# VectorE takes up four kinds of work one step later in the attention stage with heads of width 64

## The chip, the cores and the metric

The kernel runs on one core of one Trainium2 chip. The metric is the device time of the launch in microseconds; the number given for a kernel is the median of its runs.

## The reference, cut to what matters

The program computes two decoder layers on `x`, four sequences (batches) of 512 tokens of width 256. Each layer is an attention, a cross attention and a mixture of experts, each added to its input and normalised. The change lies in the fifth of these six stages, the second layer's cross attention over `ctx_1024`, with 16 heads of width 64:

```
q = (x @ Wq).reshape(b, n, 16, 64)
k = (context @ Wk * 64 ** -0.5).reshape(b, m, 16, 64)
v = (context @ Wv).reshape(b, m, 16, 64)
attn = softmax(einsum('bihd,bjhd->bhij', q, k))
out = einsum('bhij,bjhd->bihd', attn, v).reshape(b, n, 1024) @ Wo + bo
x = layernorm(x + out)
```

Four batches and 512 queries, 512 keys each.

## The kernel before, in words

The stage is the function `cross_heads`. It goes through 4 batches x 16 heads x 4 tiles of 128 rows, so 256 *steps* `s`, 64 to a batch (`STEPS`). Each engine has its own instruction list, written by its own loop `for s in range(FIRST, LAST)`, and works it off in order. Engines meet only at semaphores. Within a step the order of an engine's work is the order of the blocks in its loop.

A product in float32 quality is made of three passes over operands that are split in two: `hi` is the value rounded by ScalarE as it copies it, `lo` is what VectorE finds by subtracting `hi` from the value. The pairs are `srcp` (the batch's x, turned), `ctxp` (the context), `V_hi`/`V_lo`, and for each head `qs`, `q2`, `ks`, `k2`.

What TensorE (PE) does in step s, in this order (lines 1940 to 2006): the 128x512 tile of scores whose row maxima are wanted (L1955, "max(s)", into two banks in turn); the transposed scores of step s - 7 (L1965, L1966); the weighted sum of step s - 10, three matmuls (L1979 to L1981); every fourth step a transpose of four columns of maxima (L1990); and then work that comes at few steps of a batch only:

- turning x, two chunks, at steps 56 and 57 of the batch before (L1910, "turn(0)" and "turn(1)"), bank SPARE
- the products for V, `VALUES` (L1904): two at step 0 and two at step 2 (one in SPARE, one in ROW_BANK), then one each at steps 9, 10, 16, 17 in SPARE
- the products for q (steps 3, 11, ..., 59, bank SPARE) and for k (steps 5, 13, ..., 61, bank ROW_BANK) of the next two heads (L1904)
- the output product with Wo, `OUTS` (L1937), in SPARE, half of the heads and half of the rows at a time: at steps 58, 65, 88 and 89 counted from the batch's start, so at steps 58 of the batch and 1, 24 and 25 of the next

SPARE and ROW_BANK are one PSUM bank each, so the next product in a bank waits for VectorE to have taken the one before: `PE.wait_ge(SPARE.free, SPARE.use(...))`. The transpose L1990 goes to ROW_BANK too.

ScalarE (ACT) makes in a step the two exponentials of step s - 7 (L2043, L2047), then every fourth step the copies `raw` (L2055) and `rowbuf` (L2062), then the `hi` parts: context (L2068, at step 54), x (L2073), V (L2080), q and k (L2090, L2092).

GpSimd (POOL) subtracts `hi` from the exponentials (L2198, one in every step), copies q (L2204), and at steps 46 to 49 adds the bias (L2210).

VectorE (DVE) has in step s, in this order (lines 2104 to 2184): the row maxima of max(s) (L2111), which wait for PE's matmul; `V_lo` (L2123); `ctxp` low (L2127); `srcp` low (L2132); the low parts of q and k (L2141, L2144); the reciprocal (L2151, steps 1, 5, 9, ...); the scaling of the attention by it, `attT` (L2159, steps 0, 4, 8, ...); the addition of an output product to `summed` (L2169); the statistics and the normalisation of the layer.

Before the change, VectorE takes up V_lo, ctxp low, srcp low and the addition L2169 in the same step in which PE and ACT produce what they read. VectorE's list then waits there, ahead of max(s + 1). The step is chosen by one number, `of_batch(s, r)`, which gives the batch for which s is step r.

PE starts a head's first max matmul (L1955, j == 0) once half of its q and k low parts (`SPARE.free_at`, `ROW_BANK.free_at`), POOL's copy of q and a DMA of ks (L2243, issued by SP) are done.

Of the kernel before, what the change touches and what calls it, by code (L numbers as in the profile page):

```python
# [121 lines left out]
def plain(ap):  # L122
    return ap.bitcast(f32)
# [1686 lines left out]
def cross_heads(kit):  # L1810
# [11 lines left out]
    STEPS = H1 * TB  # L1822
# [4 lines left out]
    with ExitStack() as ph:  # L1827
# [51 lines left out]
        def place(u):  # L1879
            return u // STEPS, u // TB % H1, u % TB  # L1880

        def of_batch(s, r):
            b, x = divmod(s - r, STEPS)
            return b if x == 0 and 0 <= b < B else None
# [214 lines left out]
        def dve():  # L2099
# [4 lines left out]
            for s in range(FIRST, LAST):  # L2104
                if 0 <= s < END:
                    b, h, j = place(s)
# [10 lines left out]
                        V.wait_ge(weighed.sem, weighed[u - NHI])  # L2117
                    V.tensor_tensor(STp[u % NHI][1], ST[u % NFULL], plain(STp[u % NHI][0]), ALU.subtract).then_inc(low["dve"].sem, low["dve"].inc(u))
                for r, t, n, bk in VALUES:
                    b = of_batch(s, r)  # L2120
                    if b is not None:
                        V.wait_ge(v_high.sem, v_high[b, t, n])
                        V.tensor_tensor(V_lo[:, t, n * N:(n + 1) * N].rearrange("p (h f) -> p h f", f=HD), bk.ap.rearrange("p (h f) -> p h f", f=HD), plain(V_hi[:, t, n * 8:(n + 1) * 8, 0:HD]), ALU.subtract).then_inc(bk.free, 1)  # L2123
                b = of_batch(s, 54 - STEPS)
                if b is not None:
                    V.wait_ge(ctx_high.sem, ctx_high[b])
                    V.tensor_tensor(ctxp[1], ctxT, plain(ctxp[0]), ALU.subtract).then_inc(ctx_low.sem, ctx_low.inc(b))  # L2127
                for c in range(DC):
                    b = of_batch(s, 56 + c - STEPS)
                    if b is not None:  # L2130
                        V.wait_ge(src_high.sem, src_high[b, c])
                        V.tensor_tensor(srcp[1][:, c, :], SPARE.ap, plain(srcp[0][:, c, :]), ALU.subtract).then_inc(SPARE.free, 1)  # L2132
                for r, of, half in ((4, "q", 0), (6, "k", 0), (7, "q", 1), (7, "k", 1)):
                    p = of_group(s, r)
                    if p is not None:
                        b, h = p[0], 2 * p[1] + half
# [9 lines left out]
                if 0 <= u < END and u % TB == 0:  # L2146
                    b, h, _ = place(u)
# [5 lines left out]
                if 0 <= u < END and u % TB == 0:  # L2153
                    b, h, _ = place(u)
# [3 lines left out]
                        V.wait_ge(SPARE.full, SPARE.full_at["outs", b - 1, h // 8, 1])  # L2158
                    V.tensor_tensor(attT[h % 2 * HD:(h % 2 + 1) * HD, h // 2, :], raw[nth(b, h) % NRAW][0:HD], rinv[h % 2], ALU.mult).then_inc(att_done.sem, att_done.inc((b, h)))  # L2159
                for r, n, z in OUTS:  # L2160
                    b = of_batch(s, r)
                    if b is not None:
                        part = summed[:, 2 * z:2 * z + 2, :].rearrange("p t d -> p (t d)")
                        V.wait_ge(SPARE.full, SPARE.full_at["outs", b, n, z])
                        if n:
                            V.wait_ge(SPARE.free, SPARE.free_at["outs", b, 0, z])
                        else:
                            V.wait_ge(based.sem, based[b, 2 * z + 1])
                        V.tensor_tensor(part, SPARE.ap, part, ALU.add).then_inc(SPARE.free, 1)  # L2169
                for t in range(TB):  # L2170
                    b = of_batch(s, STEPS + 27 + t)
# [3 lines left out]
                for t in range(TB):  # L2175
                    b = of_batch(s, STEPS + 28 + t)
# [3 lines left out]
                for t in range(TB):  # L2180
                    b = of_batch(s, STEPS + 34 + t)
# [87 lines left out]

        pe()  # L2270
        dve()
        act()
        pool()
# [477 lines left out]
```

## Time and profile before

| | us |
|---|---|
| median of 3 runs | 2060.73 (2057.05 to 2060.96) |
| the profiled execution's own time | 2050.18 |
| its span | 2048.9 |
| PE busy over the span | 1673.9 (82%) |
| DVE busy | 1166.4 (57%) |
| ACT busy | 1004.0 (49%) |
| POOL busy | 979.7 (48%) |

The stage of the change runs from about 1097 us (its first VectorE work on x and context) to 1762 us; its first max matmul (step 0 of batch 0) starts at 1109.8 us and its 256th at 1718.5 us. In this stage the matmuls overlap: one lasts 0.39 us in the records while the next starts 0.23 us after it. How far a step reaches is read from the starts of L1955, one per step.

The profiled execution took 10.55 us less than the median. It was measured by itself, and the trace can only explain its own time.

### The profile page before, as it was taken

How to read it: one execution, taken by the hardware profiler on the slowest of the kernel's cores; microseconds unless marked ns; L12 is line 12 of the kernel's file. 1: busy time of each engine (PE TensorE's matmuls, PEld its weight loads, DVE VectorE, ACT ScalarE, POOL GpSimd, SP SyncE). 2: the span in 40 equal slices, each digit the busy share in tenths (PEclk: the TensorE clock that was granted, in tenths of full speed). 3: DMA queues.
4: the chain of work that ended last, by engine and by line, in shares of the span. 5: the costliest groups of instructions: out<-in, count | busy, mean ns of one | idle time of the engine just before them, and what ended most of it. 6: DMA issues, size and time to landing. Idle time of an engine off the chain costs nothing. (4 is left out here: it accounts for less than half of the span.)

```text
span 2048.9 us, 23642 instructions
## 1 busy us (share of the span) xinstructions
PE 1673.9 (82%) x7419; PEld 1219.1 (60%) x7419; DVE 1166.4 (57%) x2253; ACT 1004.0 (49%) x1917; POOL 979.7 (48%) x824
## 2 busy tenths in 40 slices
PE   5698884999944898989974989989989998589982
PEld 2476673777832565657643656656656665466661
DVE  5656554666645686868714565565575574542224
ACT  2154442644420585858743765665665665142220
POOL 1200001343324475758750675574574675058884
PEclk9899997999975799999986999999999999679996
DMA  2300002444335223232002110020120110238776
GB/s 80 125 11 25 7 21 66 153 124 131 72 93 133 71 52 85 54 82 62 2 1 105 25 40 25 25 63 23 31 63 22 32 53 24 63 94 191 180 182 163
DMA packets 96785, 146.15 MB, mean 71 GB/s; under 512 B 22711, under 2 KB 61820, under 8 KB 93830
## 3 DMA queue, kind: packets, MB, share of 16 engines
q1 hardware_dynamic: 65104, 102.69, 17.5%
q0 software_dynamic: 18432, 26.36, 7.1%
q10 hardware_dynamic: 13126, 15.60, 2.5%
q8 instruction: 61, 1.00, 0.2%
q14 instruction: 62, 0.51, 0.1%
HBM read 101.83 MB, written 36.41 MB: 67 GB/s over the span
## 5 line engine op out<-in xcount | busy, mean ns | idle before, releaser
L2198 POOL TENSOR_TENSOR STp_lo_use<-ST_use,STp_hi_use 128x512 fp32r<-128x512 f32 x256 | 334.3, 1314 | 222.7 <-ACT ST_use L2047 221.7
L1728 POOL TENSOR_TENSOR STp_lo<-ST,STp_hi 128x512 fp32r<-128x512 f32 x192 | 248.2, 1314 | 107.9 <-ACT ST L1500 106.6
L2111 DVE TENSOR_REDUCE nmax_use<-bank 128x1 f32<-128x512 f32 x256 | 173.5, 680 | 114.9 <-PE bank L1955 110.4
L2043 ACT ACTIVATE STp_hi_use<-bank 128x512 fp32r<-128x512 f32 x256 | 152.9, 597 | 173.5 <-PE bank L1981 170.8
L1621 DVE TENSOR_REDUCE nmax<-bank 128x1 f32<-128x512 f32 x256 | 170.7, 683 | 55.7 <-PE bank L1414 55.3
L1414 PE MATMUL bank<-rows_k,rows_q 65*128 65x512 f32 x256 | 136.7, 543 | 40.0 <-DVE nmax L1621 20.8
L2047 ACT ACTIVATE ST_use<-bank 128x512 f32<-128x512 f32 x256 | 151.8, 593 | 2.4 <-POOL STp_lo_use L2198 2.4
L1497 ACT ACTIVATE STp_hi<-bank 128x512 fp32r<-128x512 f32 x192 | 116.8, 608 | 59.9 <-PE bank L1425 59.6
L1955 PE MATMUL bank<-ks,qs 128*128 128x512 f32 x256 | 111.7, 437 | 33.0 <-DMA ks<-ks 13.6
L918 POOL TENSOR_SCALAR veps<-mv 128x4 f32<-128x4 f32 x4 | 0.9, 228 | 249.8 <-DVE mv L867 249.8
L1500 ACT ACTIVATE ST<-bank 128x512 f32<-128x512 f32 x192 | 118.0, 615 | 0.0
L2628 POOL DMA_INDIRECT acc_scratch<-res,sidx_all x64 | 102.0, 1594 | 25.5 <-issue 18.3
L1965 PE MATMUL bank<-qs,ks 128*128 128x512 f32 x256 | 103.7, 405 | 7.8 <-DMA q<-rowbuf_use 7.6
L1425 PE MATMUL bank<-rows_q,rows_k 66*128 66x512 f32 x256 | 107.4, 420 | 0.8 <-ACT ST L1500 0.8
L1979 PE MATMUL bank<-STp_hi_use,V_hi 128*65 128x512 f32 x256 | 102.9, 402 | 2.8 <-POOL STp_lo_use L2198 2.8
L1966 PE MATMUL bank<-q,k 65*128 65x512 f32 x256 | 102.6, 401 | 0.0
L1981 PE MATMUL bank<-STp_lo_use,V_hi 128*65 128x512 f32 x256 | 101.8, 398 | 0.0
L1980 PE MATMUL bank<-STp_hi_use,V_lo 128*64 128x512 f32 x256 | 101.7, 397 | 0.0
L1414 PEld LDWEIGHTS bank<-rows_k,rows_q 65*128 65x128 f32 x256 | 52.2, 205 | 81.6 <-DVE nmax L1621 43.6
L2610 POOL DMA_INDIRECT rows<-tokens_scratch,gidx_all x64 | 66.3, 1037 | 63.9 <-DVE sidx_all L2502 45.0
L2597 DVE TENSOR_SCALAR res<-bank,rows 128x256 f32<-128x256 f32 x64 | 28.0, 479 | 120.1 <-DMA acc_scratch<-res,sidx_all 106.7
L1088 ACT ACTIVATE hT_hi<-bank,b 128x512 fp32r<-128x512 f32 x64 | 44.1, 689 | 94.8 <-PE bank L1007 91.3
(431 smaller groups left out, 4642.5 us busy)
## 6 DMA issues: line engine op xcount, KB each, us to landing
stage<-in_W SPq DMA_DIRECT2D x16, 1024.0 KB, 5.0
Wgu<-in_Wgu SPq DMA_DIRECT2D x32, 384.0 KB
rows_q<-hop_scratch SPq DMA_DIRECT2D x32, 256.0 KB, 4.3
ks<-ks SPq DMA_DIRECT2D x64, 128.0 KB, 2.3
rinv<-rinv_scratch SPq DMA_DIRECT2D x64, 128.0 KB, 2.9
rows_k<-hop_scratch SPq DMA_DIRECT2D x24, 256.0 KB, 5.5
hop_scratch<-qkp_hi SPq DMA_DIRECT2D x20, 256.0 KB
Wda<-in_Wdn SPq DMA_DIRECT2D x32, 128.0 KB
```

What stands on the lines that cost most here:

```text
L1414: PE.matmul(bk.ap, rows_q[0:MAX_ROW, h, j * P:(j + 1) * P], rows_k[0:MAX_ROW, h, :], start=True, stop=True).then_inc(bk.full, 1)
L1425: PE.matmul(bk.ap, rows_k[:, h, kt * P:(kt + 1) * P], rows_q[:, h, :], start=True, stop=True).then_inc(bk.full, 1)
L1497: A.activation(parts_of(u)[0], bk.ap, ACT.Exp)
L1500: A.activation(ST[u % TB], bk.ap, ACT.Exp).then_inc(bk.free, 1)
L1621: V.tensor_reduce(nmax[:, i % 2, h % HS * TB + j:h % HS * TB + j + 1], bk.ap, AX.X, ALU.max, negate=True).then_inc(bk.free, 1)
L1728: G.tensor_tensor(parts_of(u)[1], ST[u % TB], plain(parts_of(u)[0]), ALU.subtract).then_inc(low.sem, low.inc(u))
L1955: PE.matmul(bk.ap, qs[z][:, j * P:(j + 1) * P], ks[z], start=True, stop=True).then_inc(bk.full, 1)
L1965: PE.matmul(bk.ap, ks[z][:, kt * P:(kt + 1) * P], qs[z], start=True, stop=False)
L2043: A.activation(STp[u % NHI][0], bk.ap, ACT.Exp)
L2047: A.activation(ST[u % NFULL], bk.ap, ACT.Exp).then_inc(bk.free, 1)
L2111: V.tensor_reduce(nmax[:, (h % 2) * TB + j:(h % 2) * TB + j + 1], bk.ap, AX.X, ALU.max, negate=True).then_inc(bk.free, 1)
L2198: G.tensor_tensor(STp[u % NHI][1], ST[u % NFULL], plain(STp[u % NHI][0]), ALU.subtract).then_inc(low["pool"].sem, low["pool"].inc(u))
```

## The change

In VectorE's loop four blocks move to the step after the one they had. Nothing is added or taken away, and the other engines' lists are untouched.

```diff
                 for r, t, n, bk in VALUES:
-                    b = of_batch(s, r)
+                    b = of_batch(s, r + 1)
                     if b is not None:
                         V.wait_ge(v_high.sem, v_high[b, t, n])
                         V.tensor_tensor(V_lo[:, t, n * N:(n + 1) * N].rearrange("p (h f) -> p h f", f=HD), bk.ap.rearrange("p (h f) -> p h f", f=HD), plain(V_hi[:, t, n * 8:(n + 1) * 8, 0:HD]), ALU.subtract).then_inc(bk.free, 1)
-                b = of_batch(s, 54 - STEPS)
+                b = of_batch(s, 55 - STEPS)
                 if b is not None:
                     V.wait_ge(ctx_high.sem, ctx_high[b])
                     V.tensor_tensor(ctxp[1], ctxT, plain(ctxp[0]), ALU.subtract).then_inc(ctx_low.sem, ctx_low.inc(b))
                 for c in range(DC):
-                    b = of_batch(s, 56 + c - STEPS)
+                    b = of_batch(s, 57 + c - STEPS)
                     if b is not None:
                         V.wait_ge(src_high.sem, src_high[b, c])
                         V.tensor_tensor(srcp[1][:, c, :], SPARE.ap, plain(srcp[0][:, c, :]), ALU.subtract).then_inc(SPARE.free, 1)
...
                 for r, n, z in OUTS:
-                    b = of_batch(s, r)
+                    b = of_batch(s, r + 1)
                     if b is not None:
                         part = summed[:, 2 * z:2 * z + 2, :].rearrange("p t d -> p (t d)")
                         V.wait_ge(SPARE.full, SPARE.full_at["outs", b, n, z])
...
                         V.tensor_tensor(part, SPARE.ap, part, ALU.add).then_inc(SPARE.free, 1)
```

In VectorE's list each of these instructions is now behind max(s + 1) and behind what is left of step s: low parts of q and k, reciprocal, `attT`. Their own order among each other stays.

## Rows read from the trace of the kernel before

**Rows 1.** The page's costliest group: busy us, mean ns, idle before and its releaser.

```profile
L2198 POOL TENSOR_TENSOR STp_lo_use<-ST_use,STp_hi_use 128x512 fp32r<-128x512 f32 x256 | 334.3, 1314 | 222.7 <-ACT ST_use L2047 221.7
```

**Rows 2.** Windows: us, busy us of PE, PEld, DVE, ACT, POOL (instructions), clock, DMA.

```profile
1600.00:1650.00 50.00, 49.37 (x211) 34.99 (x212) 28.84 (x52) 31.82 (x63) 28.80 (x25) 1.00 0.09 22
...
1225.73:1241.70 15.97, 12.06 (x50) 8.32 (x49) 7.99 (x12) 9.02 (x17) 7.64 (x6) 0.89 0.14 35
1384.24:1400.64 16.40, 12.01 (x51) 8.47 (x49) 7.99 (x12) 9.02 (x17) 7.63 (x6) 0.90 0.14 34
1544.35:1559.21 14.86, 10.69 (x51) 7.29 (x49) 7.99 (x12) 9.02 (x17) 7.67 (x6) 1.00 0.15 36
```

**Rows 3.** Groups by line: V_lo, with its idle time before and its releaser.

```profile
L2123 DVE TENSOR_TENSOR V_lo<-bank,V_hi 128x512 fp32r<-128x512 f32 x32 | 22.1, 691 | 44.1 <-ACT V_hi L2080 44.1
```

**Rows 4.** Timeline of steps 55 and 56, batch 1: start, length, instruction, idle before.

```profile
1384.24 0.39 PE L1955 MATMUL bank<-ks,qs 128*128 128x512 f32 x1
...
1386.57 1.45 DVE L2127 TENSOR_TENSOR ctxp_lo_use<-ctxT_use,ctxp_hi_use 128x1024 fp32r<-128x1024 f32 x1 [2.58 <-ACT ctxp_hi_use L2068]
...
1387.94 0.67 DVE L2144 TENSOR_TENSOR k<-bank,ks 64x512 fp32r<-64x512 f32 x1
...
1388.82 0.47 PE L1955 MATMUL bank<-ks,qs 128*128 128x512 f32 x1 [3.03 <-issue]
...
1389.97 0.69 DVE L2144 TENSOR_TENSOR k<-bank,ks 64x512 fp32r<-64x512 f32 x1
...
1390.72 0.37 PE L1990 MATMUL bank<-ident,nmax_use 128*4 128x128 f32 x1 [0.27 <-DVE k L2144]
```

**Rows 5.** Timeline of step 62, batch 1: a max matmul and VectorE after it.

```profile
1407.98 0.40 PE L1955 MATMUL bank<-ks,qs 128*128 128x512 f32 x1
...
1408.42 0.69 DVE L2111 TENSOR_REDUCE nmax_use<-bank 128x1 f32<-128x512 f32 x1 [1.53 <-PE bank L1955]
...
1409.03 0.67 DVE L2144 TENSOR_TENSOR k<-bank,ks 64x512 fp32r<-64x512 f32 x1
```

**Rows 6.** Timeline of step 10 and the start of step 11, batch 1.

```profile
1280.74 0.39 PE L1955 MATMUL bank<-ks,qs 128*128 128x512 f32 x1
...
1281.67 0.40 PE L1980 MATMUL bank<-STp_hi_use,V_lo 128*64 128x512 f32 x1
...
1281.70 0.69 DVE L2123 TENSOR_TENSOR V_lo<-bank,V_hi 128x512 fp32r<-128x512 f32 x1 [1.25 <-ACT V_hi L2080]
...
1281.90 0.39 PE L1981 MATMUL bank<-STp_lo_use,V_hi 128*65 128x512 f32 x1
1282.44 0.50 PE L1904 MATMUL bank<-Wv_hi,ctxp_hi_use 128*128 128x512 f32 x1
...
1283.95 0.39 PE L1955 MATMUL bank<-ks,qs 128*128 128x512 f32 x1
...
1285.53 0.50 PE L1904 MATMUL bank<-srcp_hi_use,Wq_hi 128*128 128x512 f32 x1
```

**Rows 7.** Timeline: the max matmul of step 59, right behind an output product.

```profile
1400.64 0.58 PE L1955 MATMUL bank<-ks,qs 128*128 128x512 f32 x1
```

**Rows 8.** Timeline of PE, steps 1 to 5 of batch 0.

```profile
1114.41 0.62 PE L1955 MATMUL bank<-ks,qs 128*128 128x512 f32 x2
...
1114.87 0.40 PE L1904 MATMUL bank<-Wv_hi,ctxp_hi_use 128*128 128x512 f32 x1
...
1117.83 0.49 PE L1904 MATMUL bank<-srcp_hi_use,Wq_hi 128*128 128x512 f32 x1
...
1120.49 0.50 PE L1904 MATMUL bank<-ctxp_hi_use,Wk_hi 128*128 128x512 f32 x1
```

**Rows 9.** attT: all 64 (min/median/max ns), and step 48 of batch 0 with PE's idle.

```profile
L2159 DVE TENSOR_TENSOR attT<-raw,rinv x64: 673/685/5537, 1162.2 to 1745.3; 64x512 f32<-64x512 f32 x64
...
1209.32 5.53 DVE L2159 TENSOR_TENSOR attT<-raw,rinv 64x512 f32<-64x512 f32 x1
...
1215.51 0.50 PE L1955 MATMUL bank<-ks,qs 128*128 128x512 f32 x1 [3.71 <-DVE nmax_use L2111]
```

## The prediction

> **What bounds the kernel now.** The windows come first. In the middle of a batch PE is busy for 49.37 of 50 us and no other engine for more than 35 [rows 2]: here PE's list is the bound, and whatever VectorE does matters only where PE waits for it. The reader sees in the same rows the weak place: from step 55 to the start of step 59 PE is busy for 10.7 to 12.1 us of 14.9 to 16.4, three times, once in each batch that has a successor. The groups by line then show what the change is aimed at: VectorE stands idle for 44.1 us ahead of V_lo, waiting for ScalarE's V_hi [rows 3]. That is idle time of an engine that is 57% busy. It is worth something only if PE waits for VectorE because of it, so the timeline has to say where that is.
>
> It is so in one place, the weak one. In batch 1 step 55 begins at 1384.24. VectorE, still at step 54, waits 2.58 us for the context's high part and subtracts until 1388.02; only then comes the low part of k of head 14 (1387.94 to 1388.61), which PE needs for max(56). PE stood idle for 3.03 us before 1388.82. The trace says "issue", but the end of that k is what its wait names. After it the next low part of k ends at 1390.66 and the transpose in the same bank starts at 1390.72 [rows 4].
>
> **The change part by part.** No instruction is added, so all of it is a question of order.
>
> *ctxp low, step 54 to 55 (three times; before batch 0 nothing is behind it).* Low k of head 14 now goes ahead of it, and max(55) too. PE's wait of 3.03 us falls to the DMA of ks, which I put at the 0.3 us that other heads show. But ctxp low still starts when ScalarE is done, at 1386.57, and ends at 1388.02. Behind it are now low q and low k of head 15: two instructions that start 0.61 us apart [rows 5], so the second starts at 1388.55 and ends at 1389.24, and the transpose starts at 1389.3 instead of 1390.72. What is late next is thus this transpose, and of the 3.03 us only 1.4 is kept.
>
> *srcp low, steps 56, 57 to 57, 58.* From the transpose to step 59 batch 2 needs 14.86 - 6.48 = 8.4 us (its clock 1.00; 6.48 is 1390.72 - 1384.24) [rows 2, 4]. That stretch is a chain: turn(0), ScalarE's copy, low part, turn(1), copy, low part, output product. Now the maxima of the next step stand ahead of each low part, and so does attT at step 56. ScalarE is less behind, which gives some back. I add 0.6 us: 9.0. From step 55 to step 59: 5.06 + 9.0 = 14.1 us. Three times that is 42.3, against 15.97 + 16.40 + 14.86 = 47.23: -4.9 us. In the two longer ones the granted clock fell to 1.2 GHz for a while after the idle time (0.89 and 0.90 in the rows), worth some 1.3 us each. The idle time is now cut up but not gone. If both fall again the gain is 2.3. I take -3.7.
>
> *What each move costs where PE was not waiting.* SPARE is used in successive steps. PE comes to the next product in SPARE after six matmuls: 1281.90 + 0.23 - 1280.74 = 1.39 us into its step (0.23 is 1281.90 - 1281.67) [rows 6]. VectorE's maxima start 0.44 us into the step and what follows starts 0.61 after that and lasts 0.69: it ends at 1.74 [rows 5]. PE's product starts 0.05 after such an end (1281.70 + 0.69 = 2.39, product at 2.44) and its first matmul takes 0.10 more than one in a running stream (0.50 against 0.40) [rows 6]. So 1.74 + 0.05 + 0.10 - 1.39 = 0.50 us of lost PE time, in every step whose SPARE product follows one of the step before, where the old order had VectorE finished in time. In a step behind an output product the max matmul takes 0.58 for 0.39 [rows 7]; both sides move by 0.19, the cost stays. It occurs at:
>
> - step 1 (output product behind V_lo), step 2 (V behind the addition), step 3 (q behind V_lo) and step 25 (output product behind the addition), in batches 1, 2, 3: 12 times
> - step 59 (q behind the addition), batches 0, 1, 2: 3 times
>
> 15 x 0.50 = 7.5 us. The bounds of one: 0.2, if PE's sequence runs later than its records, and 0.7, a whole row maximum.
>
> *Steps 10, 11, 17.* There PE waited already, since ScalarE's V_hi comes late in the step: the products start 1.70 and 1.58 us into it [rows 6] and will start at 1.79. So 0.1 + 0.2 + 0.2 a batch, four batches: 2.0 us.
>
> *Batch 0, steps 1 to 3.* There are no scores yet, so PE runs up to VectorE at once. V_lo of the first product now ends at 1114.41 + 1.74 = 1116.15, and the third V product starts at 1116.2 instead of 1114.87. Six and six matmuls later, step 3 starts near 1119.0, and its q product at 1119.0 + 1.79 = 1120.8 instead of 1117.83. A wait of some 0.3 for the transpose is then gone: the k product comes at 1123.2 for 1120.49 [rows 8]. 2.7 us; bounds 1.3 and 4.
>
> *Covered moves.* ROW_BANK's V_lo (steps 1 and 3) are free before steps 2 and 4 want them. The last batch's additions come after the last max matmul. The low parts before batch 0 have no maxima to go behind. SP and POOL wait only for ctxp low among the moved, 50 steps later. If the cover of the ROW_BANK ones failed, each would cost another 0.6.
>
> **Sum.** 7.5 + 2.0 + 2.7 - 3.7 = +8.5 us. The profiled execution took 2050.18, so the changed one would take 2058.7. That execution is 10.55 below the median of the runs. The steps of the sum are the same in either, so the prediction is 2060.73 + 8.5 = 2069.2 us.
>
> **The rivals.**
>
> *The transition pays for all (no change).* If the transpose did not wait for the low k and the clock stayed up, step 55 to 59 would take what its matmuls need, about 11 us (busy 10.69 in batch 2 [rows 2]): 33 against 47.2, -14.2, and 12.2 - 14.2 = -2.0: 2058.7. For it: three waits of 3.03 are the largest that the change touches. Against: the ROW_BANK wait is in the code, and in rows 4 the transpose follows the end of k by 0.06.
>
> *The long attT go (faster).* In three of the four batches attT of step 48 takes about 5.5 us, where the median is 685 ns, and PE then waits 3.71 us [rows 9], and runs at 1.2 GHz for some 1.5 more. Each is worth 5.2 us. Place: step 48, where POOL has its bias additions between the subtractions. If the phase of VectorE against POOL came out otherwise, all three could vanish, as the fourth batch shows: 8.5 - 15.6 = -7.1, 2053.6. From the second one on the sum is below zero. Against: from step 26 to step 54 no instruction is moved, and PE sets the pace.
>
> *More long attT (slower still).* At steps 0, 16 and 56 attT stood behind V_lo or srcp low; now it comes right after the maxima, when POOL is in L2198, which it is for 1314 ns in every step [rows 1]. If attT is caught as at step 48, each costs up to 4.86 us (5.53 - 0.67), of which a long step such as 0 or 16 covers about half. One each in three batches is some +8: 2077. The Trainium skill ("SBUF — State Buffer", Who interferes with whom) says that a VectorE instruction with two SBUF inputs contends with a GpSimd instruction that reads SBUF, and that the later of the two blocks until the first has finished. By that rule attT waits for one L2198, which the trace has at 1314 ns, and the three moves would cost little; the 5.53 us of rows 9 is longer than one such wait, so the trace is harsher than the rule here.
>
> **How the numbers follow.** The forecast (+5 to +12) has 0.63, no change 0.16, the long attT gone 0.09, more of them 0.12. A measurement here tells 0.2%, 4.1 us, from no change. Slower: 0.63 + 0.12, plus a little of the second: 0.76; same 0.15; faster 0.09. Bounds: 15 x 0.2 and 15 x 0.7 for the main term, 1.3 and 4 for batch 0, -2.3 and -8 for the transitions; cut to eight in ten, with the runs' own scatter of 4 us: 2059.5 to 2077.
>
> **What would show it.** Right: the wait of 3.03 us before step 56 is 0.3, and the transpose behind it starts 5.1 us after step 55; V_lo ends 1.74 us into steps 1, 3, 10, 11, 17 with the maxima before it; steps 1, 2, 3, 25 and 59 are 0.50 longer each; PE's waits named after V_lo and summed grow from under 1 to some 7 us, while VectorE's idle 44.1 us ahead of V_lo shrinks to almost nothing. Wrong: steps 1 to 3 of their old length, step 55 to 59 under 13 us, or attT of step 48 at 0.7 us in all batches.

## The result, and the profile after

The changed kernel takes 2069.39 us (median of 22 runs, 2053.11 to 2072.24) against 2058.69 for the kernel before (22 runs, 2051.76 to 2069.18). The ratio is 1.0042, with a 95% interval of 1.0028 to 1.0056: slower by about 9 us (6 to 12); +8.5 was forecast. (The two medians by themselves are 10.7 us apart.)

The two profiled executions differ by 12.1 us of span (2061.0 against 2048.9). Between the first and the last max matmul (L1955) the stage went from 608.74 to 618.60 us, +9.9. The other 2.2 us lie in stages whose instructions are the same. Over all eleven profiled executions of this document what lies outside the stage takes 1440.1 to 1450.4 us, with no instruction of it changed, and the kernel before has the shortest. So stages and steps are compared here, and not spans.

The starts of L1955 give the length of each step, and the steps of both kernels can be laid side by side. Outside the steps of the prediction nearly all agree within 0.05 us; the exceptions are steps 43 to 52, where a DMA or attT lands differently from run to run (+0.3 us in sum).

| steps | before | after | difference | forecast |
|---|---|---|---|---|
| 1, 2, 3, 25 of batches 1 to 3 | 49.7 | 56.0 | +6.3 | +6.0 |
| 59 of batches 0 to 2 | 8.9 | 10.4 | +1.5 | +1.5 |
| 10, 11, 17 of all batches | 37.2 | 39.2 | +2.0 | +2.0 |
| 0 to 5 of batch 0 | 12.2 | 15.1 | +2.8 | +2.7 |
| 55 to 58 of batches 0 to 2 | 47.2 | 44.1 | -3.1 | -3.7 |
| sum | | | +9.5 | +8.5 |

First the windows of the kernel after, as in [rows 2]: a stretch in the middle of a batch, then steps 55 to 58 of batches 0, 1, 2.

```profile
1600.00:1650.00 50.00, 48.43 (x206) 34.05 (x205) 28.37 (x45) 31.18 (x63) 29.20 (x25) 1.00 0.10 26
1222.68:1237.22 14.54, 10.71 (x50) 7.29 (x49) 8.90 (x12) 9.28 (x17) 7.63 (x6) 1.00 0.14 38
1382.27:1397.33 15.06, 12.05 (x50) 8.31 (x49) 8.97 (x12) 9.17 (x17) 7.62 (x6) 0.89 0.14 37
1546.96:1561.49 14.53, 10.66 (x50) 7.29 (x49) 8.89 (x12) 9.28 (x17) 7.61 (x6) 1.00 0.14 37
```

PE still sets the pace, with 48.43 of 50 us busy. The transitions are 14.5 us where the clock is full and 15.1 where it is not.

The timeline of steps 55 and 56 of batch 1, to be held against [rows 4]:

```profile
1382.27 0.39 PE L1955 MATMUL bank<-ks,qs 128*128 128x512 f32 x1
...
1384.12 0.47 PE L1955 MATMUL bank<-ks,qs 128*128 128x512 f32 x1 [0.30 <-DMA ks<-ks]
1384.59 1.47 DVE L2127 TENSOR_TENSOR ctxp_lo_use<-ctxT_use,ctxp_hi_use 128x1024 fp32r<-128x1024 f32 x1 [1.20 <-ACT ctxp_hi_use L2068]
1386.09 0.69 DVE L2141 TENSOR_TENSOR qs<-bank,qs 64x512 fp32r<-64x512 f32 x1
1386.82 0.69 DVE L2144 TENSOR_TENSOR k<-bank,ks 64x512 fp32r<-64x512 f32 x1
...
1387.57 0.37 PE L1990 MATMUL bank<-ident,nmax_use 128*4 128x128 f32 x1 [1.84 <-DVE k L2144]
...
1388.15 1.75 DVE L2159 TENSOR_TENSOR attT<-raw,rinv 64x512 f32<-64x512 f32 x1
```

The wait of 3.03 us before step 56 is 0.30. Of what it gave, 1.84 is given back at the transpose, behind the same subtraction of the context. The transpose starts 5.30 us after step 55.

The timeline of steps 1 to 3 of batch 2, where SPARE goes from V to the output product to V to q:

```profile
1412.91 0.39 PE L1955 MATMUL bank<-ks,qs 128*128 128x512 f32 x1
...
1413.34 0.69 DVE L2111 TENSOR_REDUCE nmax_use<-bank 128x1 f32<-128x512 f32 x1 [1.29 <-PE bank L1955]
1413.95 1.28 DVE L2123 TENSOR_TENSOR V_lo<-bank,V_hi 128x512 fp32r<-128x512 f32 x2
...
1414.68 3.72 PE L1937 MATMUL bank<-Wo_use,attT 128*128 128x256 f32 x16 [0.23 <-DVE V_lo L2123]
...
1418.05 0.58 PE L1955 MATMUL bank<-ks,qs 128*128 128x512 f32 x1
...
1419.28 0.68 DVE L2169 TENSOR_TENSOR summed<-bank,summed 128x512 f32<-128x512 f32 x1
...
1420.01 0.50 PE L1904 MATMUL bank<-Wv_hi,ctxp_hi_use 128*128 128x512 f32 x1 [0.23 <-DVE summed L2169]
...
1422.87 0.39 PE L1955 MATMUL bank<-ks,qs 128*128 128x512 f32 x1
...
1424.63 0.51 PE L1904 MATMUL bank<-srcp_hi_use,Wq_hi 128*128 128x512 f32 x1 [0.23 <-DVE V_lo L2123]
...
1426.14 0.39 PE L1955 MATMUL bank<-ks,qs 128*128 128x512 f32 x1
```

Each step has the same picture: max matmul, 0.43 us later the row maxima (0.62 behind an output product), 0.61 after that the instruction that frees the bank, and PE's product 1.76 to 1.96 us into the step with an idle time in front of it. The steps last 5.14, 4.81 and 3.27 us where they were 4.64, 4.34 and 2.75.

V_lo as the view of its line has it, for the kernel after (minimum, median and maximum ns; nothing stands under its own idle time):

```profile
L2123 DVE TENSOR_TENSOR V_lo<-bank,V_hi x32: 671/681/681, 1109.4 to 1624.1; 128x512 fp32r<-128x512 f32 x32
```

The 44.1 us that VectorE waited ahead of V_lo [rows 3] are gone altogether, as the change intends. VectorE's idle time ahead of the row maxima, spent on PE's max matmul, rose from 110.4 to 202.2 us instead. It waits for PE now, and PE waits for it more: the view of the waits has PE idle after V_lo for 6.7 us (0.2 before) and after the additions for 3.0 (0.8 before), 9.7 in all, where the prediction had some 7.

### The profile page after: what moved, and what is told of

Read it like the earlier page. It is cut to its first block and busy times, and to the rows that moved or that the text cites. A ratio compares the mean times of both kernels' runs of the same rounds, so it can differ in the third digit from the quotient of the medians.

```text
span 2061.0 us, 23641 instructions
## 1 busy us (share of the span) xinstructions
PE 1676.1 (81%) x7418; PEld 1219.1 (59%) x7419; DVE 1173.1 (57%) x2253; ACT 1003.9 (49%) x1917; POOL 982.2 (48%) x824
## 5 line engine op out<-in xcount | busy, mean ns | idle before, releaser
L2111 DVE TENSOR_REDUCE nmax_use<-bank 128x1 f32<-128x512 f32 x256 | 175.0, 684 | 207.7 <-PE bank L1955 202.2
L1955 PE MATMUL bank<-ks,qs 128*128 128x512 f32 x256 | 110.5, 433 | 25.0 <-DMA ks<-ks 13.9
L1088 ACT ACTIVATE hT_hi<-bank,b 128x512 fp32r<-128x512 f32 x64 | 44.1, 689 | 94.8 <-PE bank L1007 91.4
```

Source lines behind the costliest of these rows:

```text
L1955: PE.matmul(bk.ap, qs[z][:, j * P:(j + 1) * P], ks[z], start=True, stop=True).then_inc(bk.full, 1)
L2111: V.tensor_reduce(nmax[:, (h % 2) * TB + j:(h % 2) * TB + j + 1], bk.ap, AX.X, ALU.max, negate=True).then_inc(bk.free, 1)
```

## The experiments

All are made from one of the two kernels by moving instructions. Each was run 6 to 10 times, and the ratios are against runs of the kernel before on the same chip: for the first four experiments that is one chip (its median there 2058.96 us), for the context alone, at 57, bias apart and both another (2059.63), for the last a third (2056.68). The other columns are read from the profiled executions: first to last L1955, and the groups of steps of the table above.

| kernel | median us | ratio (95%) | stage | 1,2,3,25 | 59 | 10,11,17 | 0-5 of b0 | 55-58 |
|---|---|---|---|---|---|---|---|---|
| before | 2056.68 to 2059.63 | 1 | 608.7 | 49.7 | 8.9 | 37.2 | 12.2 | 47.2 |
| after | 2069.39 | 1.0042 (1.0028 to 1.0056) | 618.6 | 56.0 | 10.4 | 39.2 | 15.1 | 44.1 |
| V_lo alone | 2064.12 | 1.0032 (1.0009 to 1.0055) | 618.8 | 52.8 | 8.8 | 39.2 | 15.1 | 49.5 |
| additions but one | 2060.96 | 1.0010 (0.9993 to 1.0027) | 614.9 | 51.5 | 10.3 | 37.3 | 12.2 | 49.3 |
| x and context | 2054.78 | 0.9982 (0.9963 to 1.0002) | 608.3 | 49.8 | 8.8 | 37.3 | 12.2 | 45.2 |
| ahead of the maxima | 2056.73 | 1.0000 (0.9985 to 1.0016) | 605.7 | 49.7 | 8.9 | 37.2 | 12.2 | 43.6 |
| context alone | 2053.68 | 0.9971 (0.9954 to 0.9987) | 603.0 | 49.8 | 8.9 | 37.2 | 12.2 | 43.2 |
| context at 57 | 2045.48 | 0.9940 (0.9920 to 0.9961) | 598.5 | 49.8 | 8.9 | 37.2 | 12.3 | 38.9 |
| bias apart | 2039.05 | 0.9894 (0.9871 to 0.9917) | 596.8 | 49.8 | 8.8 | 37.2 | 13.3 | 49.2 |
| context at 57 and bias apart | 2024.17 | 0.9827 (0.9805 to 0.9849) | 586.9 | 49.7 | 8.8 | 37.2 | 12.2 | 38.9 |
| context at 58, bias apart | 2027.86 | 0.9852 (0.9820 to 0.9884) | 580.6 | 49.8 | 8.8 | 37.3 | 13.4 | 36.1 |

**V_lo alone.**

```diff
                 for r, t, n, bk in VALUES:
-                    b = of_batch(s, r)
+                    b = of_batch(s, r + 1)
```

> The kernel before with V_lo alone one step later. Theory (each SPARE product that follows one of the step before waits until the maxima and then V_lo are done, 0.50 us): steps 1 and 3 of batches 1 to 3 are 0.50 longer (3.1 us with batch 2's and 3's), step 2 unchanged; steps 10, 11, 17 together 0.5 longer in each batch (2.0); batch 0's steps 0 to 5 +2.8. In all +7.9 us against the kernel before (ratio 1.0038), and steps 55 to 58 unchanged at 14.9 to 16.4 us. Rival (only the sum of all moves costs, since each step's VectorE work is short by itself): under +3 us, steps 10, 11, 17 unchanged.

The groups of steps are as the theory has them: steps 1 and 3 +3.1 us, step 2 the same, +2.0 and +2.8. The median is 5 us up, the ratio 1.0032. The rival is out: the moved instruction costs at once, by itself. Steps 55 to 58 were a little longer than expected, 49.5 us. The granted clock fell there in all three batches (0.80, 0.90, 0.89), where it fell in two of three in the kernel before. The next experiment and the one on the bias, whose edits move nothing that PE waits for in these four steps, take 49.3 and 49.2 us: the 47.2 of the kernel before is the short one of four executions. PE in steps 1 and 3 of batch 2:

```profile
1421.41 0.40 PE L1955 MATMUL bank<-ks,qs 128*128 128x512 f32 x1
1423.19 3.72 PE L1937 MATMUL bank<-Wo_use,attT 128*128 128x256 f32 x16 [0.22 <-DVE V_lo L2123]
...
1430.89 0.39 PE L1955 MATMUL bank<-ks,qs 128*128 128x512 f32 x1
1432.66 0.51 PE L1904 MATMUL bank<-srcp_hi_use,Wq_hi 128*128 128x512 f32 x1 [0.23 <-DVE V_lo L2123]
```

**The additions but one.**

```diff
                 for r, n, z in OUTS:
-                    b = of_batch(s, r)
+                    b = of_batch(s, r if r == STEPS + 1 else r + 1)
```

> The kernel before with the additions of the output products one step later at steps 25, 26 and 59; the one of step 1 stays, since the low part of V two steps on would wait for it in a circle. Theory: step 25 of batches 1 to 3 is 0.59 longer as in the changed kernel (1.8 us), step 59 of batches 0 to 2 0.49 longer (1.5 us), nothing else: +3.3 us (ratio 1.0016). Rival (the cost is VectorE's total lateness): these steps below +0.2 each, since nothing else is late there; about 0.

Steps 25 and 59 are 1.7 and 1.4 us longer in sum. The stage is 6.2 us longer; what is left are steps 55 to 58 (2.1 us, the clock again) and step 9 of batch 0 (1.2 us), which the edit does not touch. The ratio of 1.0010 alone would not tell +3.3 us from nothing; the steps do. Step 25 of batch 2 begins at 1480.96 and its output product 2.06 us later, behind the addition:

```profile
1480.96 0.58 PE L1955 MATMUL bank<-ks,qs 128*128 128x512 f32 x1
1481.58 0.69 DVE L2111 TENSOR_REDUCE nmax_use<-bank 128x1 f32<-128x512 f32 x1 [2.07 <-PE bank L1955]
1482.19 0.23 DVE L2151 RECIPROCAL inverse<-folded 32x16 f32<-32x16 f32 x1
1482.35 0.62 DVE L2169 TENSOR_TENSOR summed<-bank,summed 128x512 f32<-128x512 f32 x1
1483.02 3.72 PE L1937 MATMUL bank<-Wo_use,attT 128*128 128x256 f32 x16 [0.31 <-DVE summed L2169]
```

**x and context.**

```diff
-                b = of_batch(s, 54 - STEPS)
+                b = of_batch(s, 55 - STEPS)
...
-                    b = of_batch(s, 56 + c - STEPS)
+                    b = of_batch(s, 57 + c - STEPS)
```

> The kernel before with the low parts of context and x alone one step later. Theory: only steps 55 to 58 of batches 0 to 2 change; step 55 falls from 4.6 to 1.9 us, step 56 and 57 give most of it back; 14.5 to 15.1 us for the four steps against 14.9 to 16.4, so -3.1 us (ratio 0.9985). Rival (the moves of V and the additions also slow this stretch, by putting more ahead of it): the four steps under 13.5 us, -6 us or more.

```profile
1230.42:1245.48 15.06, 12.07 (x50) 8.33 (x49) 8.98 (x12) 9.18 (x17) 7.62 (x6) 0.89 0.15 37
1387.44:1402.50 15.06, 12.09 (x51) 8.33 (x49) 8.97 (x12) 9.18 (x17) 7.63 (x7) 0.89 0.16 37
1547.73:1562.85 15.12, 12.11 (x51) 8.32 (x49) 8.97 (x12) 9.18 (x17) 7.61 (x6) 0.89 0.13 35
```

15.1 us three times (windows of steps 55 to 58), each with the clock at 0.89: it fell in every transition here and in one of three in the changed kernel. So the stretch is 14.5 us at full clock and 15.1 otherwise, whether V_lo and the additions are moved or not. In the trace the gain is 2.0 us and not the 3.1 expected. The ratio of 0.9982 is near the expected 0.9985, but its interval includes 1: the times do not show this gain.

**Ahead of the maxima.** The changed kernel, with the blocks of V_lo and of the additions taken from their places and put at the head of VectorE's step.

```diff
             for s in range(FIRST, LAST):
+                for r, t, n, bk in VALUES:
+                    b = of_batch(s, r + 1)
+                    ...
+                for r, n, z in OUTS:
+                    b = of_batch(s, r + 1)
+                    ...
                 if 0 <= s < END:
                     b, h, j = place(s)
                     bk = MAX_BANKS[s % 2]
```

> The changed kernel, with V_lo and the additions still one step later than before the change but put at the head of that step, ahead of the row maxima. Theory (the cost is that the maxima stand ahead): steps 1, 2, 3, 25, 59 return to 4.64, 4.34, 2.75, 4.84 and 2.98 us, steps 10, 11, 17 to 3.2, 3.07, 3.07, and batch 0's steps 0 to 5 to 12.2 us; steps 55 to 58 stay as in the changed kernel. So 12.6 us less than the changed kernel and 3 us less than the one before (ratio 0.9985). Rival (the cost is the later step as such): those steps stay as in the changed kernel, +0.50 each.

```profile
1415.18 0.40 PE L1955 MATMUL bank<-ks,qs 128*128 128x512 f32 x1
...
1419.83 0.58 PE L1955 MATMUL bank<-ks,qs 128*128 128x512 f32 x1
...
1424.17 0.39 PE L1955 MATMUL bank<-ks,qs 128*128 128x512 f32 x1
...
1426.91 0.39 PE L1955 MATMUL bank<-ks,qs 128*128 128x512 f32 x1
```

These are the starts of steps 1 to 4 of batch 2: 4.65, 4.34, 2.74 us, the old lengths. All four groups are back where they were, while steps 55 to 58 keep the gain. This is the decisive one: the later step by itself costs nothing, the row maxima in front, with their wait for PE's max matmul, cost it all. The stage is 13 us shorter than in the changed kernel. The expected 3 us against the kernel before shows in the trace (605.7 for 608.7) and not in the ratio, 1.0000 with an interval down to 0.9985.

**The context alone.**

```diff
-                b = of_batch(s, 54 - STEPS)
+                b = of_batch(s, 55 - STEPS)
```

> The kernel before with only the low part of the context one step later (step 55); x stays at 56 and 57. Theory: the gain of the changed kernel lies in this one move, and the move of x costs: step 55 is 1.9 us, PE's transpose in step 56 starts 5.1 us after step 55 as in the changed kernel, and from there to step 59 it takes 8.4 us as in the kernel before: 13.5 us for steps 55 to 58, three times, against 47.2 in all: -6 us (ratio 0.997), 3 us better than x and context together. Rival (x's move is neutral, since PE waits for the low k anyway): 14.5 us as in the changed kernel, -3 us.

```profile
1221.80:1235.48 13.68, 10.70 (x51) 7.29 (x49) 7.83 (x12) 9.17 (x17) 7.63 (x6) 1.00 0.15 41
1377.69:1392.93 15.24, 12.04 (x51) 8.48 (x49) 7.82 (x12) 9.05 (x17) 7.59 (x6) 0.89 0.13 36
1536.76:1551.02 14.26, 12.07 (x51) 8.37 (x49) 7.83 (x12) 9.17 (x17) 7.64 (x6) 0.88 0.15 38
```

The windows of steps 55 to 58: the one at full clock takes 13.7, as expected and 0.85 less than 14.5. The other two lose part of it to the clock. From the transpose to step 59 it takes 8.39 us there, as in the kernel before, and 9.24 in the changed kernel. So moving x costs just under 1 us per transition, by one transition at full clock, and moving the context alone is faster than the kernel before, 0.9971.

**The context at step 57, behind x.** The block of ctxp low is put behind that of srcp low and runs at step 57, while PE goes on to the output product.

```diff
-                b = of_batch(s, 54 - STEPS)
-                if b is not None:
-                    V.wait_ge(ctx_high.sem, ctx_high[b])
-                    V.tensor_tensor(ctxp[1], ctxT, plain(ctxp[0]), ALU.subtract).then_inc(ctx_low.sem, ctx_low.inc(b))
                 for c in range(DC):
...
+                b = of_batch(s, 57 - STEPS)
+                if b is not None:
+                    V.wait_ge(ctx_high.sem, ctx_high[b])
+                    V.tensor_tensor(ctxp[1], ctxT, plain(ctxp[0]), ALU.subtract).then_inc(ctx_low.sem, ctx_low.inc(b))
```

> The kernel before with the low part of the context at step 57, behind that of x, so that VectorE does it while PE is in the output product of step 58; nothing else is moved. Theory: step 55 1.9 us, and now neither max(56) nor the transpose of step 56 waits for the low k: it starts 3.3 us after step 55 instead of 5.1; steps 55 to 58 take 11.7 to 12.2 us against 14.9 to 16.4, and the clock does not fall there. -10 us in three batches (ratio 0.995). Rival (ScalarE's high part of the context, 1.06 us, still ahead of the high parts of q and k, is what holds the transpose): it starts after 4.5 us or more and the four steps take 13.5 us, -6 us.

```profile
1379.71 0.39 PE L1955 MATMUL bank<-ks,qs 128*128 128x512 f32 x1
1380.94 1.06 ACT L2068 ACTIVATE ctxp_hi_use<-ctxT_use 128x1024 fp32r<-128x1024 f32 x1
...
1382.52 0.58 ACT L2092 ACTIVATE ks<-bank 64x512 fp32r<-64x512 f32 x1
...
1383.38 0.69 DVE L2144 TENSOR_TENSOR k<-bank,ks 64x512 fp32r<-64x512 f32 x1
1384.13 0.27 PE L1990 MATMUL bank<-ident,nmax_use 128*4 128x128 f32 x1 [0.93 <-DVE k L2144]
```

The four steps take 12.98 us, three times, and the clock stays up in all three. The transpose comes 4.42 us after step 55, not the 3.3 of the theory, and the four steps miss its 11.7 to 12.2 us: ScalarE's copy of the context stands ahead of its copies of q and k, as the rival says. The size of the gain lies between the two in the trace, 8.3 us; the ratio of 0.9940 is 12 us (8 to 16), which holds the theory's 10 and not the rival's 6. Against the 49.2 to 49.5 us that three other executions took for the same twelve steps with the old order, the gain is 10.3 to 10.6.

**The bias additions apart.** On POOL, nothing on VectorE.

```diff
                 for t in range(TB):
-                    b = of_batch(s, 46 + t)
+                    b = of_batch(s, 42 + 4 * t)
```

> The kernel before with POOL's four bias additions at steps 42, 46, 50 and 54 instead of 46 to 49; no change on VectorE. Theory (attT of step 48, with two SBUF inputs, is shut out as long as POOL goes from one instruction to the next without a pause): attT of step 48 falls from 5.5 us to 1.4 or less in all batches, PE's waits of 3.7 us behind it vanish with the 1.2 GHz spell that follows, 5.2 us in each of three batches: -15 us (ratio 0.993). Rival (attT is long for another reason, its data or a DMA): it stays at 5.5 us and the time is the same.

All attT, then the one of step 48 of batch 0 (compare [rows 9]) and what POOL does meanwhile:

```profile
L2159 DVE TENSOR_TENSOR attT<-raw,rinv x64: 673/686/1432, 1164.0 to 1734.2; 64x512 f32<-64x512 f32 x64
...
1210.63 4.24 POOL L2198 TENSOR_TENSOR STp_lo_use<-ST_use,STp_hi_use 128x512 fp32r<-128x512 f32 x3 [0.39 <-ACT ST_use L2047]
...
1211.05 1.42 DVE L2159 TENSOR_TENSOR attT<-raw,rinv 64x512 f32<-64x512 f32 x1
```

For comparison POOL in the kernel before, around the attT that started at 1209.32 and took 5.53 us:

```profile
1209.17 1.29 POOL L2198 TENSOR_TENSOR STp_lo_use<-ST_use,STp_hi_use 128x512 fp32r<-128x512 f32 x1
...
1210.43 0.74 POOL L2210 TENSOR_TENSOR summed<-X,bo_use 128x256 f32<-128x256 f32 x1
1211.13 1.27 POOL L2198 TENSOR_TENSOR STp_lo_use<-ST_use,STp_hi_use 128x512 fp32r<-128x512 f32 x1
1212.37 0.71 POOL L2210 TENSOR_TENSOR summed<-X,bo_use 128x256 f32<-128x256 f32 x1
1213.05 1.25 POOL L2198 TENSOR_TENSOR STp_lo_use<-ST_use,STp_hi_use 128x512 fp32r<-128x512 f32 x1
```

POOL is in one instruction after the other without a gap until 1214.30, and attT ends 0.55 us after that. The number of the theory came true, its reason did not. With the additions apart POOL again has three subtractions in a row without a gap, from 1210.63 to 1214.87, and attT still gets in after the first of them, which ends at 1211.92; the second then takes 1.74 us instead of 1.29. So a row without a pause is not enough to shut attT out. In the long case the row holds additions between the subtractions, and POOL was busy without a gap before it too; which of these decides is open. What is shown is that the long attT end when the additions are four steps apart. With the additions apart no attT takes over 1.43 us, and steps 43 to 54 of the four batches take 106.5 instead of 121.4 us, -14.9 as expected. The times say more: 1.06% is 22 us (17 to 27), and the expected ratio of 0.993 lies outside the interval. The stage as profiled gives 11.9, since batch 0's start and the transitions were 1.1 and 2.0 us longer in this execution. The kernel before was profiled 9.5 us under its median on this chip and this one 7.5 us above its own, so the two profiles understate the difference; what makes single executions differ by that much stays open.

**Both.** The two edits together.

> Context low part at step 57 behind x, and the bias additions at steps 42, 46, 50, 54. Theory: the two gains add, since they lie at steps 48 to 51 and 55 to 58: -25 us against the kernel before (ratio 0.988). Rival (the phase between VectorE and POOL shifts and other attT are caught): attT over 2 us at other steps, and less than -18 us.

The ratio is 0.9827, -36 us (31 to 40), more than the 25 expected, as with the bias alone; in the trace the stage is 21.9 us shorter. The groups are those of the one and of the other: 38.9 us for steps 55 to 58, no attT over 1.43. The gains add in the trace. This is faster than both kernels, by 1.7% and, by the two ratios, by 2.1%.

**The context wholly at step 58.**

```diff
-                b = of_batch(s, 54 - STEPS)
+                b = of_batch(s, 58 - STEPS)
                 if b is not None:
                     A.wait_ge(ctx_in.sem, ctx_in[b])
...
-                b = of_batch(s, 57 - STEPS)
+                b = of_batch(s, 58 - STEPS)
                 if b is not None:
                     V.wait_ge(ctx_high.sem, ctx_high[b])
```

> The kernel with both (context low part late, bias additions apart), with ScalarE's high part of the context moved too, from step 54 to step 58, and VectorE's low part to step 58; both then fall beside the output product. Theory (with the low part out of the way it was ScalarE's 1.06 us ahead of the high parts of q and k of head 15 that set the transpose of step 56, at 4.41 us after step 55): the transpose starts at 3.3 to 3.6 us, steps 55 to 58 take 12.0 us instead of 12.98, -3 us in three batches against that kernel, ratio to the kernel before 0.981. Rival (another input of the transpose is late, the maxima or q's POOL copy): it stays at 4.4 us and the time is that of the kernel with both.

```profile
1372.07 0.39 PE L1955 MATMUL bank<-ks,qs 128*128 128x512 f32 x1
...
1375.54 0.27 PE L1990 MATMUL bank<-ident,nmax_use 128*4 128x128 f32 x1
```

The transpose comes 3.47 us after step 55 with no idle time shown, the four steps take 12.04 us. As to the transpose the theory holds: what held it at 4.42 us was ScalarE's copy. In time the 3 us are not shown: the expected ratio of 0.981 lies just outside the interval (0.9852, 0.9820 to 0.9884), and the times do not tell this kernel from the last one.

## Why the prediction was right, point by point

**The bound.** The prediction had PE's list as the bound and VectorE's idle time of 44.1 us worth little by itself. That is shown: all of it vanished and the kernel became slower.

**The 0.50 us.** The time from the head of the step to the product was forecast at 1.79 us and is 1.76 to 1.78 behind V_lo (1.63 in step 2 of batch 0 alone). Steps 1, 2, 3, 59: 0.50, 0.50, 0.52, 0.49 each. Step 25: 0.59. There VectorE has a reciprocal between the maxima and the addition, which the sum left out: the addition starts 0.77 us after the maxima and not 0.61 (1482.35 and 1481.58 in the rows of that step), and is itself 0.07 shorter. Twelve such steps gave 6.3 for 6.0. That it is the maxima in front, and not the later step, is shown by the kernel that puts the blocks ahead of them.

**Steps 10, 11, 17.** +0.1, +0.2, +0.2 a batch: 2.0 and 2.0.

**Batch 0.** 2.8 for 2.7, by the same two waits: counted from step 1, the third V product is 1.4 us late and the q product 3.0, as set down.

**The transitions.** -3.1 for -3.7, the term that was mis-sized most, and the nearness of the two is partly luck. Two parts of it were too short. The low q behind ctxp low starts 0.03 us after its end, where the prediction had it start a little ahead of that end, and the two low parts start 0.73 us apart, not 0.61 (1386.09, 1386.82): the transpose comes at 5.30 and not 5.06. And the rest takes 9.24 us at full clock, not 9.0: attT of step 56, now right behind the maxima, takes 1.75 to 1.77 us in all three, for 0.67 before. That this is the reason is likely, but no run moves it by itself. At full clock three times 14.54 would have been -3.6, where the prediction had -4.9; the clock, for which 1.2 us were set down, fell in one of three and cost 0.5. The one error made up for half of the other. Against the 49.2 to 49.5 us of the three other executions with the old order, this term would have been some 2 us larger, and the sum 7.4 instead of 9.5.

**The time as a whole.** 2069.2 us was forecast and 2069.39 measured. That this is met to 0.2 us is luck: the median of the kernel before, on which it was built, came out 2.0 us lower over 22 runs, and the difference of the medians 2.2 us larger than the sum.

**A slip without a price.** Of the last batch's additions only three come after the last max matmul, not all; the first one, moved from step 58 to 59, does not, but nothing waits for it there and no step of the end of that batch became longer.

**Of the rivals.** "The transition pays for all" supposed that the transpose would not wait; it waited 1.84 us. It took two more moves, low part and high part of the context both out of the way, to bring the stretch to 12.0 us. "The long attT go": they stayed, 5.52, 5.53, 5.53 us, in the same three batches, since nothing near step 48 had moved. That they go when the additions on POOL fall otherwise was right, and it was the larger prize: 15 us in the trace, with a single number on POOL. "More long attT" came true at a small price: the sum over the 64 rose from 71.3 to 79.3 us, the median from 685 to 1008 ns, but none beyond the old three took over 2 us. The Trainium skill ("SBUF — State Buffer", Who interferes with whom) has a VectorE instruction with two SBUF inputs wait for a GpSimd one that reads SBUF. The trace agrees for one such wait (1.42 us in place of 0.67), and also the other way round. In the kernel before, attT of step 48 of batch 1, the batch without a long one, starts 0.06 us ahead of POOL's subtraction, and it is POOL's that lasts longer, 1.77 for 1.29:

```profile
1372.48 0.67 DVE L2159 TENSOR_TENSOR attT<-raw,rinv 64x512 f32<-64x512 f32 x1
...
1372.54 1.77 POOL L2198 TENSOR_TENSOR STp_lo_use<-ST_use,STp_hi_use 128x512 fp32r<-128x512 f32 x1
```

In the three other batches attT of step 48 was shut out by five POOL instructions in a row, 5.0 us; a wait for one alone would not give that.

## What to carry to other kernels

An engine's idle time in front of an instruction is not the cost of its place in the list. Ask who waits for its result, and how long before he gets there: here V_lo had 1.4 us from the head of PE's step, and the maxima in front of it alone take 1.0 of these. Before moving an instruction later by a step, look where in the later step it lands; at the head it cost nothing, behind the step's first instruction 0.5 us each.

If one wait of a stretch is removed, list the other inputs of what comes next in the bound engine's list. The 3.03 us here were held by two instructions, the low part of the context on VectorE and its high part on ScalarE, each ahead of what q and k needed; the change as made kept 1.0 us a transition, all of these moves together 3.7, of which 2.8 is the stretch at full clock (14.86 to 12.04) and the rest the clock.

## What the runs showed of the hardware

A VectorE instruction with two SBUF inputs can be shut out for much longer than one GpSimd instruction lasts: 5.53 us for 0.67, over five GpSimd instructions in a row, additions and subtractions in turn. It was so in three of four batches in each of the eight kernels that have the additions at steps 46 to 49. Spread four steps apart, the same additions did not do this, and every attT took 1.43 us or less, also where GpSimd's subtractions followed each other without a gap. What decides is not shown.

TensorE's granted clock fell to 1.2 GHz in some of the transitions, and in others of the same instructions it did not (0.89 and 1.00 in the windows above): in 11 of 12 with the old order, which has 4.2 us of idle time in 14.9 at full clock; in 4 of 9 with the order of the changed kernel (3.9 in 14.5), three of them in one execution and none in another; in 2 of 3 with the context alone moved (3.0 in 13.7). It cost 0.5 to 1.6 us each time, and 2.2 to 2.4 in the three where it stayed down longest (0.80). With the context at step 57 (2.3 in 13.0) it fell in none of six, and at 58 (1.4 in 12.0) in none of three.
